# Subtraction and both exponentials on pairs of key groups, 2048 columns an instruction, in a GroupNorm attention kernel

## What is computed

```python
x = x + _L0_conv_ref(_gn(x), Wq, Wk, Wv, gamma)
# with v = _gn(x), reshaped to (4, 256, 4096):
f = jnp.einsum('qc,bcn->bqn', Wq, xf)          # 64 channels
g = jnp.einsum('qc,bcn->bqn', Wk, xf)          # 64 channels
h = jnp.einsum('vc,bcn->bvn', Wv, xf)          # 256 channels
scores = jnp.einsum('bqn,bqm->bnm', f, g)
beta = jax.nn.softmax(scores, axis=1)          # over n
o = jnp.einsum('bvn,bnm->bvm', h, beta)
out = gamma[0] * o + xf
```

## Time and profile before

| | us |
|---|---|
| median of 3 runs (1971.37 to 1973.39) | 1973.11 |
| the profiled execution | 1974.76 |
| its span in the trace | 1973.0 |
| PE busy in it | 1899.5 |
| DVE, ACT, POOL busy in it | 1617.9, 1590.3, 1299.8 |

### The profile page before, as it was taken

One profiled execution on the slowest core, in us unless ns is written; L12 is line 12 of the kernel. 1 busy time (PEld: TensorE's weight loads), 2 busy tenths in 40 slices (PEclk: granted clock), 3 DMA queues, 4 the chain that ended last, 5 costly groups with the idle time before them and its releaser, 6 DMA issues. The chain is left out here.

```text
span 1973.0 us, 44069 instructions
## 1 busy us (share of the span) xinstructions
PE 1899.5 (96%) x17476; PEld 1565.3 (79%) x17476; DVE 1617.9 (82%) x1961; ACT 1590.3 (81%) x1699; POOL 1299.8 (66%) x746
## 2 busy tenths in 40 slices
PE   2889999999999999999999999999999999999999
PEld 1578888887788888888777888888878788888887
DVE  7778899888777899897876889998787778878784
ACT  3588888988777888898876888889887688888885
POOL 2066767876546766887554677688655476676776
PEclk9899999999999999999999999999999999999999
DMA  3012212211112121221110221121111011111111
GB/s 110 12 31 73 75 23 54 73 31 23 49 23 69 46 75 30 61 67 23 47 25 17 74 73 54 24 75 53 30 41 32 18 33 33 23 32 31 32 32 35
DMA packets 193629, 86.97 MB, mean 44 GB/s; under 512 B 149137, under 2 KB 186257, under 8 KB 193425
## 3 DMA queue, kind: packets, MB, share of 16 engines
q1 hardware_dynamic: 193424, 84.16, 16.2%
HBM read 46.60 MB, written 16.78 MB: 32 GB/s over the span
## 5 line engine op out<-in xcount | busy, mean ns | idle before, releaser
L310 POOL TENSOR_TENSOR PL<-SC,PH 128x1024 f16<-128x1024 f32 x512 | 1091.3, 2137 | 636.3 <-ACT SC L524 634.3
L416 PE MATMUL O<-V,PH 128*128 128x257 f16 x4096 | 1119.9, 273 | 9.4 <-POOL PL L310 5.2
L418 PE MATMUL O<-V,PL 128*128 128x257 f16 x4096 | 1119.8, 273 | 0.0
L417 PE MATMUL O<-V,PH 128*128 128x256 f16 x4096 | 1118.1, 273 | 0.0
L523 ACT ACTIVATE PH<-SC 128x1024 f16<-128x1024 f32 x512 | 540.6, 1056 | 134.3 <-PE O L418 121.6
L714 DVE TENSOR_TENSOR SC<-SC,MB 128x1024 f32<-128x1024 f32 x512 | 614.9, 1211 | 0.4
L517 ACT ACTIVATE SC<-S 128x1024 f32<-128x1024 f32 x512 | 502.5, 1012 | 124.5 <-issue 106.2
L674 DVE TENSOR_TENSOR XM<-S,XM 128x1024 f32<-128x1024 f32 x384 | 468.1, 1219 | 130.6 <-PE S L404 129.2
L524 ACT ACTIVATE SC<-SC 128x1024 f32<-128x1024 f32 x512 | 534.8, 1044 | 0.0
L416 PEld LDWEIGHTS O<-V,PH 128*128 128x128 f16 x4096 | 406.6, 99 | 59.2 <-DVE OSB L750 6.0
L417 PEld LDWEIGHTS O<-V,PH 128*128 128x128 f16 x4096 | 401.3, 98 | 50.7
(11 more groups left out here) (84 smaller groups left out, 1138.5 us busy)
## 6 DMA issues: line engine op xcount, KB each, us to landing
xin<-x SPq DMA_DIRECT2D x24, 1024.0 KB, 5.9
xres<-x SPq DMA_DIRECT2D x64, 256.0 KB, 2.9
out<-RES SPq DMA_DIRECT2D x64, 256.0 KB, 2.2
ATT<-OT SPq DMA_DIRECT2D x1008, 16.0 KB, 1.9
SC<-x SPq DMA_DIRECT2D x4, 1024.0 KB, 8.7
GG<-GG SPq DMA_DIRECT2D x32, 128.0 KB, 2.4
SC<-wvT SPq DMA_DIRECT2D x1, 256.0 KB, 9.4
SC<-wqT SPq DMA_DIRECT2D x2, 64.0 KB, 10.5
```

The lines of the kernel that those rows point to most:

```text
L310: pool.tensor_tensor(PL[:, s % RING, :], sc(s), PH[:, s % RING, :], ALU.subtract).then_inc(pl_ready, 1)
L416: mm(o[:, 0:C + 1], PH[:, n % RING, cols], vh, start=t == 0, stop=False)
L417: mm(o[:, 0:C], PH[:, n % RING, cols], vl, start=False, stop=False)
L418: w = mm(o[:, 0:C + 1], PL[:, n % RING, cols], vh, start=False, stop=t == T - 1)
```

## The change

`subtract` and `exps` take two groups, 2048 columns, in one instruction; they are called at even n only. The subtraction of a pair still comes four groups ahead (it then covers n + 4 and n + 5). The exponentials come two groups ahead and cover n + 2 and n + 3, so `EXP_LEAD` goes from 3 to 2; they wait for the same count of weighed groups, n, as before. POOL's `low_weights` still takes one group at a time, and by `EXP_LEAD` it now stands at n + 2 in POOL's loop, in place of n + 3.

```diff
-    EXP_LEAD = 3
+    EXP_LEAD = 2
...
+        def sc2(s):
+
+            k, g = divmod(s, G)
+            first = (k % 2) * T * M + g * GW
+            return SC[:, first:first + 2 * GW]
+
...
             def exps(s):
-                act.wait_ge(sub_ready, s + 1)
+
+                act.wait_ge(sub_ready, s + 2)
                 if s >= RING:
-                    act.wait_ge(weighed, s - RING + 1)
-                nc.scalar.activation(PH[:, s % RING, :], sc(s), ACT.Exp, bias=SHIFT)
-                nc.scalar.activation(sc(s), sc(s), ACT.Exp, bias=SHIFT).then_inc(exp_done, 1)
+                    act.wait_ge(weighed, s - RING + 2)
+                nc.scalar.activation(PH[:, s % RING:s % RING + 2, :].rearrange("p r w -> p (r w)"), sc2(s),
+                                     ACT.Exp, bias=SHIFT)
+                nc.scalar.activation(sc2(s), sc2(s), ACT.Exp, bias=SHIFT).then_inc(exp_done, 2)
...
-            for s in range(EXP_LEAD):
-                exps(s)
+            exps(0)
...
-                if n + EXP_LEAD < K * G:
+                if n % 2 == 0 and n + EXP_LEAD < K * G:
                     exps(n + EXP_LEAD)
...
             def subtract(s):
                 k = s // G
                 dve.wait_ge(mb_ready, k + 1)
-                dve.wait_ge(s_stored, s + 1)
-                tile = sc(s).rearrange("p (i m) -> p i m", i=GT)
-                ve.tensor_tensor(tile, tile, MB[:, 0:M].unsqueeze(1).to_broadcast([P, GT, M]),
-                                 ALU.subtract).then_inc(sub_ready, 1)
+                dve.wait_ge(s_stored, s + 2)
+                tile = sc2(s).rearrange("p (i m) -> p i m", i=2 * GT)
+                ve.tensor_tensor(tile, tile, MB[:, 0:M].unsqueeze(1).to_broadcast([P, 2 * GT, M]),
+                                 ALU.subtract).then_inc(sub_ready, 2)
...
-            for s in range(SUB_LEAD):
+            for s in range(0, SUB_LEAD, 2):
                 subtract(s)
...
-                if n + SUB_LEAD < K * G:
+                if n % 2 == 0 and n + SUB_LEAD < K * G:
                     subtract(n + SUB_LEAD)
```

## The result

The changed kernel takes 2156.3 us (median of 4 runs, 2155.1 to 2157.4) against 1973.3 before: a ratio of 1.093, 95% interval 1.091 to 1.095, so 183 us slower. The forecast was 2134, between 2095 and 2172. The profiled execution has a span of 2153.3, 180.3 above that of before.

The account below looks back on a forecast made before the run. PE was taken as the bound, meeting a PE-ACT-DVE chain without slack at the small product. Ordinary tiles 133, projection tiles 20, start 3 and tail 5 add 161 us: 2134 us, 8% slower, range 2095 to 2172.

Parts of the forecast that it names:

- The bound and the chain: PE bounds the kernel; its stream and a PE-ACT-DVE-PE chain meet at the small product, 12.3 us into each tile, without slack.
- The prices: A wide exponential takes 1.81 us start to start, a wide subtraction 2.19; joining saves 0.10 a pair on ACT, 0.06 on DVE.
- The first rival: Saved fixed parts of the joined instructions reach PE, capped by its waits at 16 us: 1957 us; chance 0.02.
- The ordinary tile: First fold at 5.08 us, small product at 15.02; PE stands 2.71 us in each of 49 tiles, 133 us.
- The cover: POOL's low half of g = 1, some 1.4 us late in 12 tiles after a `low_input`, is swallowed by the DVE chain.
- tail: Groups 496 to 511, without scores: PE waits for exponentials and POOL, 1 us four times, POOL additions about 1; 5 us.
- Start: The first wide subtraction and exponentials make PE start 2.8 us later, which swallows tile 0's chain.
- Tiles with projections: 12 tiles (j = 13, 14, 15, 0) lose 1.7 us on average, between 0 and 2.7 each; 20 us.
- the clock: Rival: the granted clock falls after the wait in each of 49 tiles, 1.55 us each, 76 on top, 2210 us; chance 0.05.
- The signs: Changed profile: PE near 89% with busy time unchanged, 50 to 60 small-product waits of 2.5 to 3 us, clock still 0.99.
- Half (b): Rival: the exponentials' shift is off the path, only the subtraction's 1.06 us counts; 73 us, giving 2046; chance 0.06.
- every pair (c): Rival: wide instructions cost over 0.34 us a pair more, so g = 4 and g = 6 stall too; 2208 us; chance 0.05.

## Why the prediction was right, and where it was off

**The bound and the chain: right.** PE's stream and the chain PE, ACT, DVE, PE met at the small product with nothing to spare, and the run with the subtraction ahead of the first fold found 0.12 us a tile to be had there already.

**The prices: right.** 1.81 from start to start for a wide exponential was 1.82 (779.97 to 781.79), 2.19 for a wide subtraction was 2.19. The run with narrow instructions in the same places puts the saving of the width at 0.31 us a tile. So the rule of the Trainium skill ("VectorE: DVE Perf Modes", section on the TRN2 errata), that one large tile pays the fixed latency once, holds here. The first rival, that this saving reaches the time, is refuted by that run: it is real and an order smaller than what the grouping costs.

**The ordinary tile: right.** First fold at 5.08, small product at 15.02, 2.71 us forecast; 5.08, 15.02 and 2.71 measured. Its parts are borne out by the runs in which one part is absent: with the narrow exponentials in their old place 1.02 is left, with the copy between them 0.91. The parts don't simply add, though: with the exponentials wide alone the tile lost 2.93, by the loop from ACT to DVE and back. The wide subtraction's place breaks that loop. I had looked at chains through PE only and had not seen it; the changed kernel's forecast came out without it because the loop is absent there, not because it had been ruled out.

**The cover: right, with its reason.** POOL's late low halves after a `low_input` were swallowed by the longer wait, as forecast; in tile 8 PE waits 1.4 us for POOL, and then 1.0 in place of 2.1 at the small product:

```profile
PE O L422 <- POOL PL L316: 1.4, 1, 1.4
PE S L431 <- ACT SC L523: 1.0, 1, 1.0
```

Where the longer wait was taken away, they came to light and cost up to 3 us a tile.

**Smaller terms.** Ordinary tiles: 133 forecast, 128 measured; tail 5 and 4.8. Start 2.8 and 3.6: PE's first weigh comes 2.80 later (107.68), as forecast, and tile 0, said to be swallowed, adds the rest. Tiles with projections 20 and 22, but this agreement is luck: with the clock taken out, j = 13 is 3.6 longer and j = 0 2.7 to 3.3, more than the most that was allowed, while j = 15 is 0.4 longer (1.0 forecast) and j = 14 0.2 to 0.6 (1.1 to 1.4).

**The term that was mis-sized: the clock.** The forecast took the granted clock as unchanged and had its fall in every tile as a rival at 0.05. It fell in 15 stretches of 63, against two others before: net 13 x 1.65 = 21 us, where the forecast had nothing. That is more than the whole miss between the profiled executions (161 forecast, 180.3 measured; the ordinary tiles took 5 back); the 3 us more between 2134 and 2156 are where these two executions lie among their runs. The price per fall was right (1.55 forecast from the earlier trace rows). Wrong was the choice between "like 5.25 us of waiting" and "like 2": 2.7 us was sometimes the one and sometimes the other. And the row taken for "like 2" was one execution's chance. The changed kernel has the same wait of 2.00 us there, up to 87.92, and its clock fell behind it:

```profile
85.00:90.00 5.00, 3.00 (x22) 0.85 0.01 2
```

It fell there in 10 of the 13 kernels of this document (the kernel before and the runs with `share_maxima` late and with the changed kernel's subtraction first are the three others). The falls go with the longest single wait of a tile by the profile, and not with what the tile loses. With the exponentials alone wide an ordinary tile loses 2.93 us, but in waits of at most 1.7, and the clock fell in none of the 49; the seven falls of that run are in tiles with projections, behind waits of 2.1 to 4.3. In the changed kernel it fell in 13 of the 37 ordinary tiles with a wait of 2.05 and in none of the 12 after a `low_input`, where POOL splits the wait and no part is over 1.7. With narrow instructions in place, at 2.2 in nearly all, it was 8 of 49. Why it falls in one tile and not in the next, which look alike, no run here was made to settle.

**The signs.** PE's share, the lengths of the wide instructions and the first fold's wait came as foretold. The small product shows 50 waits of up to 2.1 us, 86 in all, in place of 2.5 to 3 and some 150, since the page counts from the modelled end and part of the delay stands at the scores of g = 2. PE's busy time was to be unchanged and rose by 38 us, 21 of it the clock (tile 18 has 29.36 busy, tile 19 27.70), and the mean clock was 0.983, not 0.99.

**Half (b), every pair (c):** the first is excluded by the first fold's wait of 3.16 us for the copy; the second did not occur in the changed kernel, where PE waits at the scores 0.4 us in one pair of four, and no more. With the exponentials wide alone two pairs of four did run slower than PE's 6.79 us, on ACT and DVE; PE felt it only at the next small product.

## What to carry to other kernels

Before joining two instructions, ask what stood between them and who waits for it: here a copy behind exponentials that grew from 1.9 to 3.6 us, and a fold behind a subtraction that grew from 1.1 to 2.2, cost the bound engine 2.7 us a round while both their engines became less busy. Lay out one round with starts and releases relative to the bound engine, follow every semaphore that a join waits for, not the last one only, and look for loops between two other engines that need not pass the bound one. A wait that hides another makes that other free; count what comes to light before pricing the repair.

## What was not expected of the hardware

The TensorE clock fell to half behind some waits of the same length and not behind others. Of the 37 ordinary tiles with a 2.05 us idle stretch of PE (2.3 us between starts of products), 13 had a little over 3 us at 0.50 of full speed and took 1.65 us longer, and the others stayed at 1.00. Behind one and the same wait of 2.00 us early in the program it fell in 10 of 13 kernels. So one execution whose clock stayed up behind a wait of this length doesn't show that it will.
